# Attention's ramp: two u stores and one query/key store issued earlier, and one set of norm reciprocals computed before batch 0's weights

## The reference

```
Q, K, V = x Wq + bq, x Wk + bk, x Wv + bv          # 8 heads of 16 channels
qq, kq  = Q Wc2q + bc2q, K Wc2q + bc2q             # 8 numbers a head, per token
qn, kn  = norm(qq), norm(kq)
fid     = (qq . kq) / max(qn kn, 1e-8)             # a cosine
qw      = fid (1 + 0.1 sin(pi fid))
aw      = 0.5 qw + 0.5 (Q . K) / sqrt(16)
probs   = softmax(aw);  heads = probs V
```

## Time and profile before

| | before |
|---|---|
| median of runs (lowest to highest) | 507.27 us (504.33 to 507.42) |
| profiled execution, and its span | 505.17 us, 503.4 us |
| busy: PE, DVE, ACT, POOL | 377.1, 372.5, 333.4, 245.3 us |
| share of the chain that ended last | DVE 39%, PE 33%, issue 11%, DMA 5%, POOL 4%, ACT 3% |
| batch 2's first weight to batch 3's | 103.18 to 115.12 |
| clock granted to PE over the span | 0.884 of full speed |

### The profile page before, as it was taken

How to read it: one execution, slowest core, us unless ns; L and a number is a source line. 1 busy time by engine, 2 the same in 40 slices (tenths; PEclk the granted TensorE clock), 3 DMA queues, 4 the chain that set the end, 5 groups by cost and what they waited for, 6 DMA issues and landing times.

```text
span 503.4 us, 8868 instructions
## 1 busy us (share of the span) xinstructions
PE 377.1 (75%) x2644; PEld 264.6 (53%) x2644; DVE 372.5 (74%) x910; ACT 333.4 (66%) x635; POOL 245.3 (49%) x348
## 2 busy tenths in 40 slices
PE   1967368899999999998888898640004599999960
PEld 0755236566656666665575336440003488888840
DVE  5496587799999999999965344997982057776781
ACT  1357347699999999999866456656203287778730
POOL 7469131755555555554201224216477147766773
PEclk9998758799999999999888999976557599999995
DMA  9416344366776776676599910000128346766400
GB/s 203 16 31 158 94 90 106 97 166 165 169 174 149 175 182 170 163 170 158 143 134 146 148 22 1 2 0 23 35 73 247 106 119 198 206 208 195 136 14 0
DMA packets 87979, 60.33 MB, mean 120 GB/s; under 512 B 17213, under 2 KB 80705, under 8 KB 87926
## 3 DMA queue, kind: packets, MB, share of 16 engines
q1 hardware_dynamic: 78022, 52.07, 46.9%
q10 hardware_dynamic: 7408, 3.35, 2.7%
q0 software_dynamic: 2496, 4.29, 2.4%
HBM read 35.38 MB, written 25.21 MB: 120 GB/s over the span
## 4 chain that ended last, share of the span: by engine, by line
DVE 39%; PE 33%; issue 11%; DMA 5%; POOL 4%; ACT 3%; SPq 2%; ACTq 1%; POOLq 0%; DVEq 0%
DVE big L1850 11%; DVE mxs L1827 10%; PE ps L1635 8%; PE ps L1626 7%; DVE big L1880 4%; PE ps L1418 2%; PE ps L1431 2%; PE ps L1528 2%; PE ps L1523 1%; PE ps L1411 1%; PE ps L1223 1%; DVE u_sb L1889 1%; DMA qk_parts<-proj 1%; DVE gb L1698 1%; DMA uk_parts<-u_turned 1%
## 5 line engine op out<-in xcount | busy, mean ns | idle before, releaser
L1850 DVE SCALAR_TENSOR_TENSOR big<-big,ps 128x1024 f32<-128x1024 f32 x64 | 74.2, 1215 | 4.4 <-ACT big L954 4.4
L1827 DVE TENSOR_REDUCE mxs<-ps 128x4 f32<-128x1024 f32 x64 | 74.1, 1216 | 4.5 <-issue 2.8
L954 ACT ACTIVATE big<-ps 128x1024 f32<-128x1024 f32 x64 | 62.4, 1028 | 11.3 <-PE ps L1396 11.1
L842 POOL DMA_INDIRECT out_dram<-arena,fidx x46 | 46.5, 1010 | 25.3 <-DVE arena L2246 17.9
L2218 DVE TENSOR_SCALAR arena<-ps,x_all 128x128 f32<-128x128 f32 x46 | 14.0, 347 | 46.3 <-PE ps L1643 34.4
L1626 PE MATMUL ps<-arena,big 128*128 128x256 f32 x184 | 45.4, 392 | 1.1 <-issue 1.1
L1635 PE MATMUL ps<-arena,big 128*128 128x256 f32 x184 | 45.8, 393 | 0.5 <-ACT arena L1162 0.5
L1144 ACT ACTIVATE x_all<-x_all 128x128 f32<-128x128 f32 x46 | 20.3, 489 | 37.0 <-DMA x_all<-sorted_rows 30.1
L1258 PE MATMUL ps<-arena 96*128 96x256 bf16 x256 | 39.3, 285 | 7.2 <-issue 4.8
L828 POOL DMA_INDIRECT sorted_rows<-proj,sl_i x32 | 32.6, 1020 | 21.9 <-issue 15.5
L1880 DVE TENSOR_TENSOR big<-big,ps 128x1024 f32<-128x1024 f32 x32 | 37.9, 1216 | 6.9 <-PE ps L1418 6.9
(11 more groups left out here) (350 smaller groups left out, 893.0 us busy)
## 6 DMA issues: line engine op xcount, KB each, us to landing
big<-in_L_ffn_w_dram SPq DMA_DIRECT2D x34, 256.0 KB
qk_parts<-proj SPq DMA_DIRECT2D x16, 384.0 KB, 3.0
arena<-qk_parts SPq DMA_DIRECT2D x32, 192.0 KB, 3.7
sorted_rows<-zrow SPq DMA_DIRECT2D x16, 266.0 KB, 5.7
arena<-qk_parts SPq DMA_DIRECT2D x32, 128.0 KB, 3.9
big<-in_L_ffn_w_dram ACTq DMA_DIRECT2D x12, 256.0 KB
x_all<-sorted_rows SPq DMA_DIRECT2D x23, 133.0 KB
sorted_rows<-zrow SPq DMA_DIRECT2D x2, 1263.5 KB, 24.5
```

Source lines behind the costliest of these rows:

```text
L842: nc.gpsimd.indirect_dma_start(out2, bass.IndirectOffsetOnAxis(ap=fidx[:, j, t:t + 1], axis=0), fres[j][:, t, :], None, bounds_check=NT * ...
L954: nc.scalar.activation(W[par][:, n, :], src, ACT.Sin, scale=PI * (1 - 1e-6)).then_inc(sin_ready, 1)
L1827: nc.vector.tensor_reduce(mxs[:, b1 % 2, :, 2 * n:2 * n + 2], src, AX_X, ALU.max, negate=True).then_inc(unit_free, 1)
L1850: nc.vector.scalar_tensor_tensor(W[par][:, n, :], W[par][:, n, :], 10.0, f, ALU.add, ALU.mult).then_inc(unit_free, 1)
```

## The change

On SP, the store of u of batch 1 moves ahead of the load of u of batch 0, and the store of the third queries and keys ahead of the load of u of batch 1. On DVE, the reciprocals of part 1 move from behind the tops of batch 2 to before the first weight of batch 0. Nothing is added or removed.

```
             put_u(0)
+            put_u(1)
             get_u(0)
-            put_u(1)
+            put_qk(2)
             get_u(1)
-            put_qk(2)
             get_qk(2)
             put_max(0)
             get_max(0)
...
                     for n in range(HP):
                         top(1, n)
+                    reciprocals(1)
...
                     for n in (3, 2, 0, 1):
                         top(b + 2, n)
-                if first:
-                    reciprocals(1)
```

## The result

The changed kernel took 504.46 us in the median of 20 runs (501.16 to 508.01), the kernel before 507.45 in 20 runs beside it (504.33 to 509.47). The ratio is 0.9942 with a 95% interval of 0.9923 to 0.9960, a gain of 2.9 where 5.1 was forecast. The sign and the steps behind the branch were right. At the branch 2.7 were lost, where 0.5 had been allowed.

A forecast was written before the change was run, and what follows sets the result against it. The prediction took waits before 103.18, from SP's queued maxima store and DVE's reciprocal, as the bound, with DVE busy afterwards. Gain 5.6 less 0.5 at the branch made 5.1; 506.05 - 5.1 = 501.0, range 498.7 to 504.8.

The forecast's parts named there:

- the steps behind the branch: Waits in batches 0 and 1 after the branch, followed one by one: 5.6 gained in all up to batch 2's first weight.
- the term for the branch: At the branch, queries and keys on DMA beside instruction loads: 0.5 lost, between nothing and 3.3.
- The base: Starting time for the forecast: 506.05, the average of four times of the kernel before.
- So this costs nothing: SP's queue: two loads of u and their dependents now behind the queries-and-keys store; needed at 67.9 or later, so no cost.
- Batch 0's term: In batch 0, the second logit on DVE starts at 79.28 and not 79.73: 0.45 gained.
- The reciprocal's old place: Before batch 1's weights on DVE: 1.8 gained at its first weight, then 3.4 more within batch 1.
- POOL's root: On POOL, the root runs from 77.85 to about 81.5 without idling first, instead of 88.01 to 91.6.
- The branch pays more: Rival at the branch: PE leaves up to 3.3 later, gain 2.3, time 503.8; chance 0.13.
- The sign set on PE's exit: Sign at the branch: the prediction is wrong if the branch ends later than 61.97 by more than 1.
- the half clock in batch 1: Rival on PE: clock falls in batch 1 as before, gain 3.8, time 502.3; chance 0.15.
- the late rise: Rival on PE: clock stays half to the end of batch 1, 6.5 lost, time 507.5; chance 0.07.
- The reciprocal that only changes place: Rival on DVE: reciprocal's cost and return of 2.46 cancel, only POOL's 1.35 remains, time 504.7; chance 0.10.

The follow-up runs named there:

- e6: Changed kernel with each load of u for batches 0 and 1 cut into four of 32 partitions, same order and bytes; ratio to the kernel before 0.9897.
- e3: Changed kernel with store and load of the third queries and keys moved behind the first store of the maxima; ratio to the kernel before 0.9914.
- e7: e4 plus three extra 128 KB loads of x behind the first u's load, source written as 4 groups of 32 rows; ratio to the kernel before 0.9933.
- e8: e4 plus the same three extra loads at the same place, source written as one run of 128 rows; ratio to the kernel before 0.9868.
- e1: Kernel before with SP's new order alone, the reciprocal at its old place; ratio to the kernel before 1.0029.
- e2: Kernel before with the reciprocal alone moved, SP's order as before; ratio to the kernel before 0.9896.
- e4: Changed kernel with batch 1's u and the third queries and keys all behind the first store of the maxima; 501.67 us, ratio to the kernel before 0.9897.
- e5: Changed kernel with only the load of the second u moved behind the first store of the maxima; ratio to the kernel before 0.9878.

## Why the prediction was wrong

- **The failed step is the term for the branch.** I allowed 0.5, between ends of 0 and 3.3, because the branch before already ran beside the second u's packets. It measured 2.71, near the upper end. I also read it at the wrong engine: by the flag PE goes on only 0.39 later, but DVE, whose way out of the branch I did not look at, goes on 3.59 later (7.70 against 4.11). With 2.71 the forecast's own sum holds: 5.6 - 2.71 = 2.89, against 2.88 to batch 2 by the flag and 2.9 by the ratio of the runs. e6, which has the new order with the loads of u in pieces, and the branch as before, comes to batch 2 5.54 sooner, where 5.6 was forecast without the branch. The nearest row was the wrong one to lean on: what ran there before was a store of u, and what the change brought in were two loads of u with the store of queries and keys between them, and loads of u are worked off by few engines (e3, e7 against e8). The better row was at hand: the store that took 6.30, which I read as crowding, had a quarter of its packets behind a load of u.
- **The base was low too.** 504.46 lies 3.5 above the forecast of 501.0. The gain accounts for 2.1 of that (3.0 between the medians, 5.1 forecast), and the base for 1.4: I started from 506.05, and 20 runs of the kernel before have a median of 507.45.
- **The reason given for the branch term was half right.** That data could delay instruction loads was named. The prediction cited the Trainium skill's page DMA: Bandwidth & Descriptors, section "Queues, rings and completion order", for queue rows served in turn, a packet at a time. By that rule alone I would expect a wait of about a packet. The measurement differs. The runs show the first load on queue 14 start 1.9 to 3.5 later than in the kernel before while loads in four groups are under way, and on time when the same bytes are spread (e8) or pieces at a like share arrive (e6). So a backlog on few engines is what delays it, and not the traffic as such; how it does so is not shown. The load on queue 8 came in every case, at most 0.6 later.
- **"So this costs nothing", said of SP's order, held for the waits on the queue only.** Nobody waited for the loads that stand later. The price was paid on DVE, and e1 shows that alone it outweighs the earlier maxima (47.33 against 46.28).
- **Batch 0's term** of 0.45 can be read from tops to second logit: 13.05 in the changed kernel (81.13 - 68.08), 13.48 before (79.73 - 66.25), 0.43 less. The first logit was released by the second weight, as said.
- **The reciprocal's old place** gave back what was worked out. From the second logit to batch 1's first weight it is 6.33, where it was 8.12: 1.79 less, 1.8 forecast. From there to batch 2's first weight it is 11.96, where it was 15.33: 3.37 less, 3.4 forecast. POOL's root began at 79.64 without a wait before it, and batch 1's logits waited for nothing.
- **The rivals and the signs.** "The branch pays more" is nearest to what happened; it had 0.13, with 503.8 as its time, and the median came at 504.46. But it had PE up to 3.3 later, which PE was not, and its time is near in part by luck: its gain of 2.3 was 0.7 too small and its base 1.4 too low. The sign set on PE's exit (later than 61.97 by more than 1) did not show, since it watched the wrong engine; batch 0's second logit did come later than 79.73, at 81.13. The clock stayed full through batch 1 (1.00 from 81.30 to 99.42), so neither the half clock in batch 1 nor the late rise happened. The reciprocal that only changes place fell with e2.

Left open is which DMA engine an instruction load uses, since the trace doesn't record it, and so by what step a backlog on about four engines holds the loads of queue 14 back for 2 to 3.5 us. Nor is it tested what as long a backlog on all 16 engines would do.

## What to carry to other kernels

A transfer that is moved earlier is to be costed where its packets land in time, not only for who waits on its queue: look for a branch or the first use of new code there. Read the DMA share as a number of engines, too: a low, flat level such as 0.28 may be a few engines with a backlog, and a source written as a few large groups made one here (e7 against e8). The share alone doesn't say so, as e6 shows; look at which packets come late. In a change of two parts run each alone: here one part gained 1.0%, the other took some of it back, and an order of the same stores and loads that leaves the branch quiet kept it all (e4).

## What the runs showed of the hardware that was not expected

Three loads of 128 KB ahead of the branch made its tops 2.55 later (11.69 in e7, 9.14 in e4 without them) or 0.25 (9.39 in e8), depending on how the source's rows were grouped. Two loads of u in four groups held the DMA share at 0.28 in e3, at 97 GB/s, for three us, and a quarter of the packets of a store issued behind such a load came late (192 of 768 in e5). And from the flag to DVE's first instruction behind the branch it takes 4.24 even with no data moved from 1.5 to 4.5 after the flag (60.18 - 55.94 in e4), of which DVE idles 2.88.
